# A recommendation tower on one core: eight features looked up by matmul and nineteen gathered, and the layers cut in three parts

## The reference, cut to what matters

```python
e = jnp.stack([tbl_0[ids[:, 0]], ..., tbl_26[ids[:, 26]]], axis=1)      # 512 x 27 x 128
z = jnp.einsum('bfd,bgd->bfg', e, e)[:, _TRIL_I, _TRIL_J]               # 512 x 351
h = jnp.concatenate([z, dense_ctx], axis=1)                             # 512 x 367
h = jnp.maximum(h @ W_top1 + b_top1, 0.0)                               # 367 x 512
h = jnp.maximum(h @ W_top2 + b_top2, 0.0)                               # 512 x 256
y = h @ W_top3                                                          # 256 x 1
```

## Time and profile before

| | us |
|---|---|
| three runs | 137.06, 139.27, 139.56 |
| median | 139.27 |
| the profiled execution: its time | 137.53 |
| its span in the trace | 135.7 |
| PE busy | 127.3 (94%) |
| POOL busy | 65.2 (48%) |
| DVE busy | 73.0 (54%) |
| ACT busy | 35.1 (26%) |

### The profile page before, as it was taken

How to read it: one execution, slowest core, us unless ns; L and a number is a source line. 1 busy time by engine, 2 the same in 40 slices (tenths; PEclk the granted TensorE clock), 3 DMA queues, 4 the chain that set the end, 5 groups by cost and what they waited for, 6 DMA issues and landing times.

```text
span 135.7 us, 2307 instructions
## 1 busy us (share of the span) xinstructions
PE 127.3 (94%) x954; PEld 76.5 (56%) x954; DVE 73.0 (54%) x129; ACT 35.1 (26%) x73; POOL 65.2 (48%) x75
## 2 busy tenths in 40 slices
PE   0699999999999999999999999899999999989993
PEld 0244344435444443545445454589898988877860
DVE  4799994919669293874919500084656450411121
ACT  4000304004050320505013050565537262020210
POOL 3877777787778777777877777700000000000000
PEclk9999999999999999999999999999999999999999
DMA  3899999522122112212221221200000000000000
GB/s 39 268 385 386 390 347 317 149 79 56 48 58 58 48 51 58 58 39 58 58 52 45 63 58 39 58 19 7 5 5 0 5 5 0 0 0 0 0 0 1
DMA packets 6706, 11.23 MB, mean 83 GB/s; under 512 B 3438, under 2 KB 3950, under 8 KB 6696
## 3 DMA queue, kind: packets, MB, share of 16 engines
q1 hardware_dynamic: 3448, 6.63, 14.2%
q0 software_dynamic: 2176, 4.46, 11.9%
q10 hardware_dynamic: 1072, 0.00, 0.4%
HBM read 11.09 MB, written 0.00 MB: 82 GB/s over the span
## 4 chain that ended last, share of the span: by engine, by line
PE 92%; DMA 3%; DVE 1%; ACT 1%; issue 1%; SPq 1%
PE ps_l L178 52%; PE ps_g L214 11%; PE ps_l L251 8%; PE ps_x L194 6%; PE ps_x L271 5%; PE ps_i L226 5%; DMA early<-in_tbl_look 3%; PE ps_i L168 2%; PE ps_g L284 2%; PE ps_i L238 1%; ACT ET L440 1%; DVE h2T L388 1%; SPq L131 0%; SPq L130 0%; DVE y_sb L394 0%
## 5 line engine op out<-in xcount | busy, mean ns | idle before, releaser
L156 POOL DMA_INDIRECT X<-in_tbl,ids_all x68 | 64.3, 946 | 22.2 <-issue 19.8
L178 PE MATMUL ps_l<-onehot,early 128*128 128x512 f32 x160 | 72.3, 606 | 0.9 <-DMA early<-in_tbl_look 0.9
L355 DVE TENSOR_SCALAR onehot<-ps_i,vocab 128x512 f32<-128x512 f32 x80 | 53.4, 743 | 19.3 <-PE ps_i L168 19.3
L178 PEld LDWEIGHTS ps_l<-onehot,early 128*128 128x128 f32 x160 | 30.3, 195 | 36.6 <-issue 29.3
L440 ACT COPY ET<-ps_l 128x512 f32<-128x512 f32 x10 | 10.6, 1055 | 67.9 <-PE ps_l L178 67.9
L367 DVE COPY early<-ps_g 26x208 f32<-26x208 f32 x32 | 11.6, 364 | 18.4 <-PE ps_g L214 17.3
L214 PE MATMUL ps_g<-ET 128*58 128x52 f32 x512 | 15.9, 218 | 0.6 <-ACT ET L440 0.4
L214 PEld LDWEIGHTS ps_g<-ET 128*58 128x58 f32 x512 | 14.6, 133 | 2.0 <-DVE early L367 0.7
L451 ACT COPY early<-ps_g 26x208 f32<-26x208 f32 x32 | 10.4, 326 | 10.7 <-PE ps_g L214 10.2
L251 PE MATMUL ps_l<-ZT,w 128*128 128x256 f32 (+1 forms) x48 | 10.9, 383 | 0.0
L251 PEld LDWEIGHTS ps_l<-ZT,w 128*128 128x128 f32 (+1 forms) x48 | 8.9, 189 | 1.7 <-issue 0.4
(11 more groups left out here) (23 smaller groups left out, 17.3 us busy)
## 6 DMA issues: line engine op xcount, KB each, us to landing
early<-in_tbl_look SPq DMA_DIRECT2D x10, 512.0 KB, 9.4
X<-in_tbl,ids_all POOLq DMA_INDIRECT x68, 2.5
w<-in_W_top SPq DMA_DIRECT2D x2, 256.0 KB
w<-in_W_top SPq DMA_DIRECT2D x1, 512.0 KB, 16.0
w<-in_W_top SPq DMA_DIRECT2D x1, 222.0 KB
ids_all<-in_ids SPq DMA_DIRECT2D x1, 54.0 KB, 2.1
Z<-in_dense_ctx SPq DMA_DIRECT2D x1, 32.0 KB, 13.8
ids_l<-in_ids_look SPq DMA_DIRECT2D x1, 20.0 KB
```

Of the source, the lines that this page charges most:

```text
L156: pool.indirect_dma_start(out=X[:, t % 2, at, :], out_offset=None, in_=tables[f][:, :], in_offset=bass.IndirectOffsetOnAxis(ap=ids_all[:, ...
L178: last = pe.matmul(ps_l[f % 2][:, 0:batch], tbl[:, f, c, :], onehot[:, f % RING, c, :], start=(c == 0), stop=(c == CHUNKS - 1))
L355: dve.tensor_scalar(onehot[:, f % RING, c, :], ps_i[f % 2][:, 0:batch], vocab[:, c:c + 1], None, ALU.is_equal).then_inc(onehot_ready, 1)
```

## The change

`LOOKED` loses features 23 and 24, which are gathered now. That makes 8 features looked up and 19 gathered, in groups of 4, 4, 4, 4 and 3 a tile, still twenty groups. `G` is kept for three tiles at a time in a ring instead of for all four; DVE and ACT wait with the first products of tile 3 until `lay(0)` is done. The layers run in three parts, of 256, 128 and 128 samples. The second layer writes to `ps_l` instead of `ps_x`, and the third to a free part of `ps_l[1]` instead of `ps_g`, so that they can stand between turns and products. The second layer finishes one output block before it begins the other. The groups of tile 3 are copied by DVE when their number is even.

The order on PE is written out anew. Twelve groups are turned among the eight look-ups. The other eight are turned among the products of tiles 0 to 2 and the first two parts of the layers; products of tile 3 and the third part of the layers stand at the end.

The diff, cut to its core (the order on PE in full; DVE and ACT follow it):

```diff
-LOOKED = [0, 3, 6, 9, 14, 17, 20, 21, 23, 24]
-GATHERED = [[1, 2, 4, 5], [7, 8, 10, 11], [12, 13, 15], [16, 18, 19], [22, 25, 26]]
+LOOKED = [0, 3, 6, 9, 14, 17, 20, 21]
+GATHERED = [[1, 2, 4, 5], [7, 8, 10, 11], [12, 13, 15, 16], [18, 19, 22, 23], [24, 25, 26]]
...
-HALVES = 2
+G_RING = 3
+
+PARTS = [(0, 2), (2, 3), (3, 4)]
+WIDEST = 2 * P
...
-    return n == TURNS - 2
+    return n >= 3 * GROUPS and n % 2 == 0
...
-        early = sb("early", [P, SIDE * batch])
+        early = sb("early", [P, G_RING * SIDE * P])
...
+            def first_layer(n):
+
+                start, end = parts[n]
+                w = end - start
+                pe.wait_ge(zt_kept, end // P)
+                if n == 0:
                     pe.wait_ge(w1_in, len(k1) * DMA)
                 else:
-                    pe.wait_ge(h1_act, half1)
-                    pe.wait_ge(h1_dve, half1)
+                    pe.wait_ge(h2_act, n)
                 for m in range(m1):
+                    if n and m == half1:
+                        pe.wait_ge(y_kept, n)
...
+            def second_layer(n):
+
+                start, end = parts[n]
+                w = end - start
+                if n == 0:
                     pe.wait_ge(w2_in, DMA)
...
+                pe.wait_ge(h1_act, (n + 1) * half1)
+                for m in range(m2):
+                    for c in range(m1):
+                        if m == 0 and c == half1:
+                            pe.wait_ge(h1_dve, (n + 1) * half1)
+                        last = pe.matmul(ps_l[m][:, 0:w], w2[:, c, m * P:(m + 1) * P], h1T[:, c, 0:w],
+                                         start=(c == 0), stop=(c == m1 - 1))
+                    last.then_inc(h2_done, 1)
...
             products(0, 0)
             products(0, 1)
-            turn(TURNS - 2)
             products(0, 2)
-            turn(TURNS - 1)
             products(0, 3)
+            turn(12)
             products(1, 0)
             lay(0)
             products(1, 1)
             turn_z(0)
             products(1, 2)
+            turn(13)
             products(1, 3)
+            turn(14)
             products(2, 0)
             lay(1)
             products(2, 1)
             turn_z(1)
+            turn(15)
             products(2, 2)
             products(2, 3)
+            first_layer(0)
+            turn(16)
+            lay(2)
+            second_layer(0)
+            turn(17)
+            turn_z(2)
+            third_layer(0)
+            first_layer(1)
+            turn(18)
+            turn(19)
+            second_layer(1)
             products(3, 0)
-            lay(2)
             products(3, 1)
-            turn_z(2)
+            third_layer(1)
             products(3, 2)
             products(3, 3)
-            first_layer(0)
             lay(3)
-            second_layer(0)
             turn_z(3)
-            third_layer(0)
-            first_layer(1)
-            second_layer(1)
-            third_layer(1)
+            first_layer(2)
+            second_layer(2)
+            third_layer(2)
...
             def keep_products(t, r):
 
                 dve.wait_ge(dots, t * QUARTERS + r + 1)
+                if r == 0 and t >= G_RING:
+                    dve.wait_ge(z_laid, t - G_RING + 1)
...
```

More of the change, by code:

```diff
@@ L62, in build @@
     half1 = m1 // 2
-    wide = batch // HALVES
+    parts = [(a * P, b * P) for a, b in PARTS]
     assert n_in == pairs + n_dense and m2 == 2 and m1 == 4 and batch == TILES * P
@@ L255, in first_layer, with third_layer @@
                         last.then_inc(h1_done, 1)
-            def second_layer(h):
-                if h == 0:
+            def second_layer(n):
+                start, end = parts[n]
+                w = end - start
+                if n == 0:
                     pe.wait_ge(w2_in, DMA)
[L261 to L279, removed]
+                pe.wait_ge(h1_act, (n + 1) * half1)
[6 more added lines that the diff above has]
+                    last.then_inc(h2_done, 1)
+            def third_layer(n):
+                start, end = parts[n]
+                w = end - start
+                if n == 0:
                     pe.wait_ge(small_in, 3 * DMA)
-                pe.wait_ge(h2_act, h + 1)
-                pe.wait_ge(h2_dve, h + 1)
+                pe.wait_ge(h2_act, n + 1)
+                pe.wait_ge(h2_dve, n + 1)
                 for c in range(m2):
-                    last = pe.matmul(ps_g[0][0:1, h * wide:(h + 1) * wide], w3[:, c:c + 1], h2T[:, c, :],
+                    last = pe.matmul(ps_l[1][0:1, WIDEST:WIDEST + w], w3[:, c:c + 1], h2T[:, c, 0:w],
                                      start=(c == 0), stop=(c == m2 - 1))
@@ L292, in _ @@
             pe.wait_ge(ident_ready, 1)
[L293 to L299, removed]
+            look_up(0)
+            spread_ids(2)
+            turn(0)
+            look_up(1)
+            spread_ids(3)
+            turn(1)
+            turn(2)
+            look_up(2)
+            spread_ids(4)
+            turn(3)
+            look_up(3)
+            spread_ids(5)
+            turn(4)
+            turn(5)
+            look_up(4)
+            spread_ids(6)
+            turn(6)
+            look_up(5)
+            spread_ids(7)
+            turn(7)
+            turn(8)
+            look_up(6)
+            turn(9)
+            turn(10)
+            look_up(7)
+            turn(11)
             products(0, 0)
             products(0, 1)
-            turn(TURNS - 2)
             products(0, 2)
-            turn(TURNS - 1)
             products(0, 3)
+            turn(12)
             products(1, 0)
@@ L408, in _ @@
             keep_products(0, 1)
-            keep_turned(TURNS - 2)
             keep_products(0, 2)
@@ L457, in keep_zt, with keep_h1, keep_h2 @@
                          ps_i[1][:, 0:len(k1) * P].rearrange("z (c p) -> z c p", c=len(k1))).then_inc(zt_kept, 1)
[L459 to L463, removed]
+            def keep_h1(n):
+                w = parts[n][1] - parts[n][0]
+                act.wait_ge(h1_done, n * 2 + 1)
+                if n:
+                    act.wait_ge(h2_done, m2 * n)
                 for m in range(half1):
-                    act.activation(h1T[:, m, :], ps_l[0][:, m * wide:(m + 1) * wide], ACT.Relu, bias=b1[:, m:m + 1]) \
+                    act.activation(h1T[:, m, 0:w], ps_l[0][:, m * w:(m + 1) * w], ACT.Relu, bias=b1[:, m:m + 1]) \
                        .then_inc(h1_act, 1)
[L468 to L474, removed]
+            def keep_h2(n):
+                w = parts[n][1] - parts[n][0]
+                act.wait_ge(h2_done, n * m2 + 1)
+                if n:
+                    act.wait_ge(y_done, n)
+                act.activation(h2T[:, 0, 0:w], ps_l[0][:, 0:w], ACT.Relu, bias=b2[:, 0:1]).then_inc(h2_act, 1)
             act.wait_ge(numbered, 1)
@@ L481, in _ @@
                 act.dma_start(w3[:, :], W_top3.rearrange("(m p) o -> p (m o)", p=P)).then_inc(small_in, DMA)
[L482 to L486 removed]
+            keep_looked_up(0)
+            keep_turned(0)
+            keep_looked_up(1)
+            keep_turned(1)
+            keep_turned(2)
+            keep_looked_up(2)
+            keep_turned(3)
+            keep_looked_up(3)
+            keep_turned(4)
+            keep_turned(5)
+            keep_looked_up(4)
+            keep_turned(6)
+            keep_looked_up(5)
+            keep_turned(7)
+            keep_turned(8)
+            keep_looked_up(6)
+            keep_turned(9)
+            keep_turned(10)
+            keep_looked_up(7)
+            keep_turned(11)
             act.wait_ge(small_in, 3 * DMA)
```

93 lines of the change are left out of this document (51 added, 42 removed).

## The result

The changed kernel took 130.93 us (median of four runs, 130.01 to 131.49). The kernel before took 138.63 (median of four, 137.06 to 139.56). The ratio is 0.951, with an interval of 0.940 to 0.963: faster by 5%, where the forecast of 128.2 against 139.27 was 8%. The forecast's range, 125.9 to 131.8, is a ratio of 0.904 to 0.946 to the 139.27 it started from; 130.93 lies inside the times, 0.951 outside the ratios. Its profiled execution took 131.49, with a span of 129.7, and is the longest of the four; the walk had given 127.6 for it.

A forecast was written before the change was run, and what follows sets the result against it. PE's work was taken as the bound: look-ups to 70.4, products and layers to 103.95, part two to 113.8, the end to 124.2; plus 1.56 and 1.83 gives 127.6, with a third of 1.7 put back 128.2 us. Range 125.9 to 131.8.

The forecast's parts named there:

- the walk: PE's whole new order, summed from pieces of the old trace: 127.6 us for a profiled execution.
- The end, where nothing covers anything: From the last products to `y`'s copy: uncovered copies, layers and activations on tile 3, 10.4 us, to 124.2.
- The fall of the clock: Rival: PE's clock falls to 1.2 GHz; at 113.8 that gives 135, at turn 14 it gives 165; chance 0.03.
- The clock stood at 2.4 GHz throughout: Kernel before: claimed full clock all along, despite a longest PE pause of 0.7 us; used against the clock rival.
- look-ups: Start of PE's chain: eight look-ups, 57.22 us, with spreadings and turns between, end at 70.4 instead of 86.3.
- wait at turn 14: Just before products(2, 0): PE waits 0.77 us for ACT's copies of products(1, 3) and turn 14.
- Products and layers of tiles 0 to 2: After the look-ups: 18.98 us to `first_layer(0)` at 90.5, then 13.47 us, to 103.95.
- parts of 128: Layer matmuls on 128 columns: 0.115 us a record, so 2.76 for a first layer, 1.84 second, 0.6 third.
- The rival that the weight loads show: In the layers on 128 columns, weight loads add 4.0 to 5.8 us, giving 132 to 134; chance 0.10.
- gathers: On POOL: 76 at 1.25 us, last landing at 99.5, before PE reaches turn 19 at 107.3; eight more cost nothing.
- The third of the spread that I put back: Profiled execution lay 1.7 us under the median of three runs; a third added back, 127.6 to 128.2.

The follow-up runs named there:

- the filled kernel: Changed kernel plus three unused matmuls of 384, 256 and 256 columns in PE's three pauses at the end; 127.90 us, ratio 0.929 to the kernel before.
- the covered end: Changed kernel, same instructions, end reordered to cover the pauses behind the last products and `lay(3)`; median 127.42 us over six runs.
- the extra work in front: Added to the covered end with one unused matmul behind `turn_z(3)`: unused matmuls at the start on a tile filled with 1.3; 126.91 us.
- the run with identity fills: Changed kernel with three, two and two unused identity matmuls of 128 columns in PE's three end pauses; 128.10 us, ratio 0.923 to the kernel before.
- the new order alone: Changed kernel's order, but ten features looked up and seventeen gathered, as in the kernel before; 144.91 us, ratio 1.051 to the kernel before.

## Why the prediction was partly wrong

The step that failed is **"The end, where nothing covers anything"**. It priced 10.4 us from the last products to `y`'s copy, all at 2.4 GHz. It took 128.12 - 114.19 = 13.9, and of the 3.5 more, 2.6 are the first layer (5.47 against 2.88 of the same records at 104.5) and 0.44 `turn_z(3)`. The fall of the clock was among the rivals, with a chance of 0.03 and "135, still no loss" for a fall at 113.8. The mechanism was right and its place nearly so (117.4, not 113.8); the chance was far too small, and the price assumed that the clock stays down. It was down for some 7 us and cost 3.0, as the filled kernel showed by taking them back: 130.9 to 127.9. Of the 3.4 us by which the gain fell short (7.7 for 11.1) the fall is 3.0; the rest is mostly that the kernel before was 138.63 and not 139.27, and the small errors of the walk take a little of it back. The walk without the fall, 127.6 for an execution, was right to 0.3, in part by luck: in the filled kernel's trace the stretch from the first to the last products took 41.6 where the walk had 42.3, and the end 11.1 where it had 10.4.

I had set the chance by one trace of the kernel before, which has pauses up to 0.7 and no fall. One trace was too little: by the later sets that kernel's clock falls in about one execution of five. "The clock stood at 2.4 GHz throughout" was wrong as well for the first look-up, where the loads of weights are 0.86 us apart until 9.3. And I passed over that its two longest pauses of the end, 0.34 and 0.67, stand apart, with 3.5 us or more of second layer ahead of each, and that the new end puts three, of 0.86, 0.62 and 0.57, between short pieces. The changed kernel's own trace shows a fall behind those of 0.86 and 0.62, at 117.4, and none behind single ones of 0.67 and 0.80, ahead of the first products and at turn 14. That it is the short distance between the pauses that matters is argued from this, and no run changes the distance alone. The Trainium skill tells in "TensorE: Matmul & The Clock Gate", section "A second HAM failure mode: psum-queue depth-cycling", of a bf16 kernel with 512 columns that had short pauses between groups of matmuls and a clock that went back and forth. The runs here agree in that the fall came in 12 of 12 executions with the three pauses; they also show it in 5 of 17 without any. I had cited the section and let the old trace outvote it.

The other steps, by their numbers. The **look-ups**: end at 71.45 for 70.4; the difference lies in the first (9.77) and the start (6.20), which vary from run to run, and the step is right. The **wait at turn 14**: 0.80 for 0.77. **Products and layers of tiles 0 to 2**: from 72.54 to 104.52 are 31.98, for 32.45. The **parts of 128**: 2.88 and 2.68 for a first layer (in the reordered end) and 1.79 for a second, so 0.112 to 0.120 for each record, where 0.115 was taken. The rival that the weight loads show has no support; at the 0.112 to 0.120 of a record here nothing is left of the 0.05 more that an estimate by the Trainium skill's ratio of 81 to 56 ("TensorE: Matmul & The Clock Gate", section "Back-to-back issue gap") would add. The **gathers** cost nothing, and fewer look-ups in the old order cost 10 to 12 us more than before, so that this step is tested and not only argued. The third of the spread that I put back had no reason in the trace; the medians of before in two later sets were 137.97 and 138.99, and part of the spread there is the falls of its clock.

What stays open is why the clock of the same program falls in some executions and not in others, when one pause of 0.57 us is left or none, whether the short pieces of the end add to it, and what the first look-up's slow start hangs on. The lowest times are those of the covered end: medians of 127.42 without a fill, 128.30 with one, and 126.91 with one and the extra work in front, which differ by how many of the executions fell. Without a fill its executions at a clock of 1.0, at 126.4, lie 4.4 us below the changed kernel, 1.4 of it the waiting in two covered pauses and 3.0 the clock.

## What to carry to other kernels

When an order is written anew, list PE's pauses in the new order, not only its work: with a row of three pauses of 0.6 to 0.9 us, 2 us in all, the clock fell every time here and took 3 us more, and matmuls that nobody needs, put into them, gave these 3 us back in most executions. Cover them with independent work first, fill what is left, and look at the granted clock of every run for whether it held: one trace at full clock, of before or after, does not show that the next execution keeps it. And where a change has two halves, one that frees an engine and one that hides another engine behind it, either alone can be a loss (here +7 and +10 to 12 us) while both together win 7 to 8.

## What the runs showed of the hardware

The granted clock fell to 1.2 GHz and rose again within a single tail, 117.4 to about 124.2 us, with PE busy without a pause from 118.9 on. It also fell with PE busy in every window of the 30 us before (the run with identity fills, at 116.5), and did not fall after a single pause of 1.10 us (the new order alone, at 86). At the start the page's row shows full clock although the loads are 0.86 us apart, twice the 0.43 of later, so the row is silent on the first microseconds: there the distance of the loads, and the 0.34 us that each takes, are the thing to read. Work on PE ahead of the first look-up, 5 us of it with identity matmuls, did not bring the rise forward: it came near 11 us, with PE at work almost without a pause from 1.45.
